# Routing matmuls in free columns of a PSUM bank, their sums ahead of the maps' combination, and the strip copies behind the map transfers

## The reference, cut to what matters

```
x_proj = einsum('bchw,oc->bohw', x, proj_w)              # 128 -> 64 channels
att1 = route(x_proj, att1_w, att1_b, depthwise 3x3 or 5x5, dilation 1)
att2 = route(att1,  att2_w, att2_b, depthwise 7x7, 9x9 or 11x11, dilation 3)
    # route: pooled = mean over h, w; logits = pooled @ att_w.T + att_b;
    #        the convolution of the largest logit is the result
out  = concat([att1, att2], channel)
maps = concat([mean over channels of out, max over channels of out])
gate = sum over 2 of sigmoid(conv 7x7(maps, sp_w) + sp_b)
return out * gate + x
```

## Time and profile before

| What | us |
|---|---|
| median of three runs | 6009.83 |
| the profiled execution | 6016.42 |
| its span in the trace | 6014.7 |
| PE busy | 4768.7 (79%) |
| DVE busy | 3136.8 (52%) |
| ACT busy | 2827.8 (47%) |
| POOL busy | 1039.5 (17%) |

### The profile page before, as it was taken

The page is one execution under the profiler, slowest core; times in us unless marked ns, Lnnn a source line. Parts: engine busy times, 40 slices in busy tenths (PEclk is TensorE's granted clock), DMA queues, the critical chain, the costliest instruction groups (busy, mean ns, idle before and its releaser), DMA issues.

```text
span 6014.7 us, 156600 instructions
## 1 busy us (share of the span) xinstructions
PE 4768.7 (79%) x62816; PEld 3244.4 (54%) x62816; DVE 3136.8 (52%) x3931; ACT 2827.8 (47%) x5378; POOL 1039.5 (17%) x1574
## 2 busy tenths in 40 slices
PE   5678887888878888887888888788888878885453
PEld 2336474655647465564746547474654747464453
DVE  3315455554645546474554547455464755545345
ACT  3455554544545454454545454454545445451120
POOL 2001011111112111121211111121111212111232
PEclk8889999988989989898999989899998989897675
DMA  9655787979888797988879788897978888796957
GB/s 241 185 159 172 173 209 226 230 219 224 237 210 218 216 233 218 222 244 209 218 219 235 216 222 244 200 227 213 237 219 222 246 202 224 211 213 176 221 135 198
DMA packets 1033176, 1284.58 MB, mean 214 GB/s; under 512 B 670749, under 2 KB 865736, under 8 KB 1001885
## 3 DMA queue, kind: packets, MB, share of 16 engines
q1 hardware_dynamic: 899468, 723.43, 50.5%
q0 software_dynamic: 64304, 410.01, 21.8%
q10 hardware_dynamic: 69026, 146.11, 9.5%
HBM read 950.16 MB, written 456.70 MB: 234 GB/s over the span
## 4 chain that ended last, share of the span: by engine, by line
PE 50%; DMA 21%; SPq 9%; DVE 8%; issue 7%; ACT 3%; ACTq 1%; POOL 1%; another core or an unknown queue 0%; DVEq 0%; POOLq 0%
PE psC L1086 19%; PE psA L1022 10%; PE psA L1023 9%; DMA RX<-w_d 6%; SPq L439 6%; DMA RX<-in_x_dram 5%; PE psB L1054 3%; PE psA L958 3%; PE psB L1065 2%; PE psB L1032 2%; DMA out_dram<-RX 2%; DMA RX<-nat_d 2%; DVE L L1375 2%; PE psB L967 2%; DMA map_d<-RX 2%
## 5 line engine op out<-in xcount | busy, mean ns | idle before, releaser
L1086 PE MATMUL psC<-RX 61*60 61x96 f32 (+7 forms) x49152 | 1479.9, 268 | 276.1 <-POOL RX L680 129.4
L1086 PEld LDWEIGHTS psC<-RX 61*60 61x60 f32 x49152 | 1412.8, 134 | 341.9 <-issue 329.2
L875 ACT ACTIVATE L<-psC 124x120 f32 (+4 forms) x2048 | 396.8, 287 | 885.6 <-PE psC L1086 830.5
L1022 PE MATMUL psA<-X,RX 128*128 128x240 f32 x1280 | 638.0, 588 | 129.7 <-ACT RX L840 128.2
L680 POOL COPY RX<-RX 64x720 f32<-64x720 f32 x512 | 426.2, 839 | 1408.8 <-DMA RX<-w_d 1407.5
L845 ACT ACTIVATE X<-psA,bias 128x246 f32<-128x246 f32 x1024 | 626.6, 722 | 56.2 <-issue 25.6
L1054 PE MATMUL psB<-ident,L 124*128 124x124 f32 x2160 | 381.1, 318 | 334.9 <-DVE RX L1395 163.7
L1310 DVE TENSOR_REDUCE MM<-L 124x135 f32<-124x2160 f32 (+1 forms) x192 | 535.3, 2844 | 212.7 <-ACT L L875 212.7
L1395 DVE TENSOR_TENSOR RX<-psB,RX 128x360 f32<-128x360 f32 (+7 forms) x1200 | 359.2, 350 | 546.5 <-PE psB L1054 485.6
L1023 PE MATMUL psA<-X,RX 128*128 128x240 f32 x1280 | 632.5, 583 | 0.0
L865 ACT ACTIVATE RX<-L 128x1080 f32 (+1 forms) x256 | 542.4, 2127 | 147.8 <-DMA L<-strip_d 147.7
(11 more groups left out here) (122 smaller groups left out, 5008.2 us busy)
## 6 DMA issues: line engine op xcount, KB each, us to landing
RX<-in_x_dram POOLq DMA_DIRECT2D x48, 2560.0 KB, 15.2
RX<-w_d ACTq DMA_DIRECT2D x512, 180.0 KB, 4.4
RX<-in_x_dram SPq DMA_DIRECT2D x128, 720.0 KB, 9.1
out_dram<-RX SPq DMA_DIRECT2D x128, 720.0 KB, 8.4
nat_d<-X SPq DMA_DIRECT2D x320, 280.0 KB
L<-strip_d SPq DMA_DIRECT2D x192, 405.0 KB, 10.5
strip_d<-nat_d SPq DMA_DIRECT2D x48, 1440.0 KB
RX<-nat_d POOLq DMA_DIRECT2D x130, 400.0 KB, 5.1
```

What stands on the lines that cost most here:

```text
L875: ins = nc.scalar.activation(dst[:, 0:NU2 - par, 15 * r:15 * r + nq, par, :], src[:, par:BR:2, :, :], ACT.Identity)
L1022: nc.tensor.matmul(o[:, :, 0:T1], w[:, ch, 96:224], rhs, start=True, stop=False, skip_group_check=True)
L1086: ins = nc.tensor.matmul(o[:, :, 0:kk, a:b], w2t[2 * q + p][rows, ch, z:z + PB], src[rows, 2 * p + ch, 0:nf, 3 * cg + dc:3 * cg + dc + kk, ...
```

## The change

Three edits.

1. The route's matmuls write columns 400 to 450 of the bank `psC[3]`, which no other operation of that time uses, where they wrote `psA[0]`, the bank of the projection. So the matmul of the sums no longer waits until ScalarE has emptied the projection's banks (the wait for `xc_ready` goes), and it is issued before the last fill's transposes (`route_stats`, called in `project_all`) and not after them.
2. On VectorE, `combine(m)` moves from before block 5's sums to between `route_means` and `route_indices`.
3. On SP, `make_strips` of a sample is no longer the end of its own turn. It is called with `s - 1` in the next turn: behind `load_maps` in turns 2 to 16, and in turn 1 ahead of the wait for the strips.

```diff
@@ SP, turn
                 if t.two:
                     store_map2(m)
                     load_maps(m)
+                    if t.conv2:
+                        make_strips(s - 1)
                     if t.new:
                         wait_alone(sp, x_summed, NB1 * s + NB1 - 1)
...
                     sp.wait_ge(s_ones, 1)
+                    make_strips(s - 1)
                     wait_alone(sp, strip_stored, SST * s)
...
                     if t.early:
                         early_pieces(m)
-                    make_strips(s)
@@ PE, project_all
+                route_stats(s)
                 turn_x(s, *fills[-1])
+
+            def route_stats(s):
+                if isinstance(s, int) and s == 0:
+                    pe.wait_ge(psum_set, 1)
+                wait_alone(pe, stats_ready, s + 1)
+                nc.tensor.matmul(psC[3][0:C2, 400:425], projt[:, :], stats[:, :, :].rearrange("p r c -> p (r c)"),
+                                 start=True, stop=True).then_inc(stats_mm, 1)
@@ PE, route
-                pe.wait_ge(stats_ready, s + 1)
-                wait_alone(pe, xc_ready, NFS * (s + 1))
-                nc.tensor.matmul(psA[0][0:C2, 0:25], projt[:, :], stats[:, :, :].rearrange("p r c -> p (r c)"),
-                                 start=True, stop=True).then_inc(stats_mm, 1)
                 if t.two:
                     wait_alone(pe, proj_evac, NFS * (s + 1))
                     spatial(t.m, 0)
                 wait_alone(pe, pool_ready, s + 1)
-                for n, (o, m, rhs) in enumerate(((32, 2, a1t), (40, 3, a2t), (48, 3, a2t))):
-                    ins = nc.tensor.matmul(psA[0][0:1, o:o + m], pooled[:, n:n + 1], rhs[:, :], start=True, stop=True)
+                for n, (o, m, rhs) in enumerate(((432, 2, a1t), (440, 3, a2t), (448, 3, a2t))):
+                    ins = nc.tensor.matmul(psC[3][0:1, o:o + m], pooled[:, n:n + 1], rhs[:, :], start=True, stop=True)
@@ DVE, turn (route_means and route_indices read the new columns)
                 if t.new:
                     for b in range(2, NB1 - 1):
                         take_x(s, b)
-                if t.two:
-                    combine(m)
                 if t.new:
                     take_x(s, NB1 - 1)
                     stats_total(s)
                     route_means(s)
+                if t.two:
+                    combine(m)
+                if t.new:
                     route_indices(s)
```

More of the change, by code:

```diff
@@ L1230, in route_means @@
                 dve.wait_ge(stats_mm, s + 1)
-                step(nc.vector.tensor_copy(psx[:, :, :].rearrange("p r c -> p (r c)"), psA[0][0:C2, 0:25]))
+                step(nc.vector.tensor_copy(psx[:, :, :].rearrange("p r c -> p (r c)"), psC[3][0:C2, 400:425]))
                 for dst, src, ax in ((srow, psx, 0), (swin, srow, 1)):
@@ L1255, in route_indices @@
                 dve.wait_ge(logits_mm, s + 1)
-                step(nc.vector.tensor_tensor(lg[:, 0:2], psA[0][0:1, 32:34], attb[:, 0:2], ALU.add))
-                step(nc.vector.tensor_tensor(lg[:, 2:5], psA[0][0:1, 40:43], attb[:, 2:5], ALU.add))
-                step(nc.vector.tensor_tensor(lg[:, 5:8], psA[0][0:1, 48:51], attb[:, 2:5], ALU.add))
+                step(nc.vector.tensor_tensor(lg[:, 0:2], psC[3][0:1, 432:434], attb[:, 0:2], ALU.add))
+                step(nc.vector.tensor_tensor(lg[:, 2:5], psC[3][0:1, 440:443], attb[:, 2:5], ALU.add))
+                step(nc.vector.tensor_tensor(lg[:, 5:8], psC[3][0:1, 448:451], attb[:, 2:5], ALU.add))
                 l2 = lg[:, 2:8].rearrange("p (v k) -> p v k", k=3)
```

## The result

The changed kernel takes 6106.67 us (median of four runs, 6101.87 to 6123.76) against 6000.84 us for the kernel before in the same comparison: ratio 1.0183, 95% interval 1.0151 to 1.0215. It is slower by about 106 us, outside the range that was given. The profiled execution, whose rows follow, took 6123.76 us.

A forecast was written before the change was run, and what follows sets the result against it. TensorE had half the chain, DMA a fifth, neither hidden throughout. Steady turns -7.2 + 4.2 + 2.7 = -0.3 us, times 13 = -4; turn 2 +6, turns 0 and 1 -3: forecast 6007 us, range 5960 to 6075.

The forecast's parts named there:

- The strips leave the projection: Projection up to block 5: without strips ahead, block 3's load is hardly late; 7.2 us less a steady turn.
- The upper bound: Largest gain allowed for the projection: the largest wait at block 3 and the rest, 8.5 us.
- The order of the route: Block 5 to `conv1`: the combination now follows the means, so `spatial` starts later; cost 4.2 us a turn, bounds 2.5 and 6.
- T: Start of block 5 on TensorE, from which times are counted; forecast to move forward by 7.2 us, bounds 4.3 and 8.5.
- The strips' new place: Strips behind the map load: `conv1`'s weight loads land in 4.7 us, not 2.0; cost 2.7 us, bounds 0 and 6.7.
- A backlog of DMA: Sign of being wrong: strips reaching into `conv1`'s first pairs, seen as waits for `band_d` or the gate; no size given.
- The tail that I feared: Last part of the strips, still moving when `conv1`'s weight loads are issued at T+25; taken to make them land in 4.7 us.
- T+28 of the strips: Forecast end of the strips on the DMA engines: 22 us of strips plus POOL's two pieces, 1.6 MB.
- Rival C: Strips hold `conv1`'s weight loads, 8.7 us to land instead of 2.0: +3.7 us a steady turn, 6065 us; chance 0.20.
- the row at 8.7 us: Profile row before the change: weight loads landed in 8.7 us where SP's queue was full.
- The gate: Gate stored at about T+35, loaded back by T+42, before TensorE asks at T+48; cost taken as nothing.

The follow-up runs named there:

- e1: Edits 1 and 2 alone on the kernel before, strips still copied at the end of their own turn: 6103.01 us, ratio 1.0156.
- e9: Changed kernel with the piece load (first piece of x's second half, 1.4 MB) issued behind the gate's loads: 6022.95 us, ratio 1.0015.
- e2: Edit 3 alone on the kernel before, route and VectorE's order as before: 6065.82 us, ratio 1.0082.
- e7: Changed kernel with the combination between the block sums and the means: 6080.80 us, ratio 1.0098.
- e8: Changed kernel, combination between sums and means, two strip phases at their own turn's end, the third behind the next turn's maps: 5956.27 us, ratio 0.9904.
- e10: e8 with the load of the second half's first piece issued behind the gate's loads: 5939.77 us, ratio 0.9878.
- e11: e10 with one phase of strips at the end of their turn and two behind the next turn's maps: 5923.16 us, ratio 0.9847.

## Why the prediction was wrong

*The strips leave the projection:* right in mechanism. Block 3's wait fell from 5.7 to 0.7 us (0.3 forecast), the time to block 5 by 5.9 us where I had 7.2. The wait itself is 5.1 us less, where I had 5.4. (The upper bound should have been 8.3 and not 8.5: 6.83 - 0.3 + 1.8.) The stretch from block 3 to block 5, to which I gave 1.8 us, gained 1.3, partly because block 5 now waits 1.5 us for its load where it waited 1.2. The stretch before block 3 became 0.4 us longer, which I had at nothing (means over the same turns).

*The order of the route:* right in mechanism, and too small. The forecast put the sums' matmul at T+8.1, the means' end at T+11.9 and `spatial` at T+14.3. Measured were 8.4, 12.2 and 14.6 on average. The first half of `spatial`, for which I took 5.7 us, took 6.5 (4.9 before). e1 puts the price at 4.8 us at `conv1`'s start, where I had 4.2, and at 6.9 us for the whole turn.

*The strips' new place:* this is the step that failed: "I take 4.7, since the strips are in their tail by then: 2.7 us on the path". The wait grew by 6.6 us (first use 9.6 us after the issue, 3.0 before). A backlog of DMA seen as waits for `band_d` and for the gate is what the forecast had named as the sign of being wrong. The queues' traffic in the changed kernel's turn 9 shows why, from T to T+14, to T+25 and to T+35 (packets, MB, share of the 16 engines):

```profile
q1 hardware_dynamic: 1033, 4.03, 89.5%
...
q1 hardware_dynamic: 469, 2.63, 80.2%
q0 software_dynamic: 175, 0.78, 20.5%
...
q1 hardware_dynamic: 213, 1.34, 54.1%
q0 software_dynamic: 221, 0.95, 35.2%
q10 hardware_dynamic: 137, 0.27, 10.1%
```

SP's queue moved 6.66 MB until T+25, nearly all of it strips and maps. By the size of the packets 0.37 MB of the strips and 1.3 MB of the piece load were left then. The tail that I feared is the small part: in eight of the 13 turns at most 0.02 MB of the strips was left at the weights' issue, and the first use still came 6.8 to 11.3 us after it (mean 9.5; 9.8 in the five with 0.3 to 0.4 MB left). The large part is the piece load, which I had on the same queue until T+33 in the very next sentence, and POOL's two pieces, which I had counted into the T+28 of the strips; I set neither against the weights. e9 prices them: 6.1 of 7.1 us. The engines were at a share of 0.99 from T+25 to T+35. I priced a resource (who is done by then) and not the queue of work (what else has to go before a small load is served). Rival C had the size (+6.7 us on the loads) and the wrong culprit; in the row at 8.7 us on which it rests SP's queue had 67.8% of the engines from 2800 to 2850 us, and POOL's another 25.3%. With the measured terms a steady turn is -5.9 + 5.3 + 7.1 + 1.2 = +7.7 us. C had +3.7 a turn and so stopped at 6065 us: T was 1.3 us too good, the order 1.1 too cheap, the loads 0.4, and the rest of the turn, 1.2, was priced at nothing.

In whole turns the strips' move was forecast at -4.5 us. It costs 3.1 alone (e2) and 0.8 beside the other edits (the changed kernel less e1). The order was forecast at +4.2 and costs 6.9 alone (e1) and 4.6 beside the strips' move. So the sign was lost in the strips' new place, but the larger part of the loss is the order of the route, which was forecast as a cost that the strips' move would pay for.

*The gate:* "I cost that at nothing". Its loads were issued 14.1 us after its store and not 2.4, and VectorE waited 3.7 us a turn for them. TensorE's wait stayed under 1 us in the changed kernel, because `conv1` was late as well. It shows in e2 and e7, where `conv1` is earlier: 3 to 5 us a turn.

Of the Trainium skill's page that was cited, "DMA: Bandwidth & Descriptors", section "Queues, rings and completion order": that each DMA engine takes its queues in rotation did not keep the three small loads short here. In turn 9 ScalarE's queue moved its first packet 4.5 us after the issue, where it was 1.0 us before the change (3.1 on average now), 8 packets until 3145, and then 72 in 3 us:

```profile
q10 hardware_dynamic: 8, 0.02, 2.1%
...
q10 hardware_dynamic: 72, 0.14, 17.0%
```

So the loads both started late and went slowly. By the second rule (completion behind the engine's earlier writes of all queues) they would also be reported late. No run separates the two, and which part each has stays open.

## What to carry to other kernels

A bulk copy that is moved takes the whole queue behind it along: before moving it, write down every transfer that is issued after it, in its own queue and in the others, until the backlog in MB has been worked off at the measured rate, and price the small loads on the critical path against that. Copy in portions sized to the gaps, and issue loads that are needed late after the small ones that are needed now. An operation of one engine that is placed behind a wait for another engine inherits that wait: put it ahead of the wait when its inputs are there.

## What the runs showed of the hardware that was not expected

- Loads of 88 KB on a queue of their own took 2.0 us to land with the DMA engines a third busy, and 11.0 us where two other queues kept them at a share of 0.99. It made little difference that they were few and small.
- It did not matter whose queue kept the engines busy. Over turns 2 to 15 of all fourteen kernels, first use came at most 3.4 us after the issue in 133 turns, and in these SP's bulk packets had a share of at most 0.01 in the 3 us after the issue. Six turns of e8 had no more of them than that, and POOL's queue at a share of 0.94 or more: 6.7 to 7.7 us. In turn 2 of e2 it was SP's queue alone at 1.0: 7.6 us.
- What followed the bulk mattered more than the bulk itself. In e8, with 2.2 MB of strips issued 13 to 15 us before the weights, the 1.5 MB load behind them and POOL's pieces behind that cost 4 us; with that load late nothing (e10).
- After 5.3 us without a matmul the first half of `spatial` took 5.6 to 7.1 us in turns 2 to 15 of the changed kernel, at a mean granted clock of 0.56 to 0.71; after 0.93 us it took 4.00 us at 1.00 (e11). So 1.6 to 3.1 us of an idle gap's price come after its end.
